# One chunk's residual sum moved: identity matmuls and ScalarE copies in place of VectorE additions

## The chip, the core and the metric

The kernel runs on one core of a Trainium2 chip. The metric is the time of one execution on the device in microseconds (us), the median of the runs shown. The engines are TensorE (PE in the profile, its weight loads PEld), VectorE (DVE), ScalarE (ACT), GpSimd (POOL), and SyncE (SP), which only issues transfers here. "Item 2" below is the third of four chunks; chunks and halves are counted from 0, and "2.1" is chunk 2, half 1.

## The reference, cut to what matters

One layer of a language model on 2 x 1024 tokens of width 256. The token step gathers table rows and adds a low-rank correction chosen by the token's domain. Then come a recurrent attention with 16 heads of 16 x 16 states, and a quantized linear layer, each behind a layer norm and with a residual:

```
h = token_rows + 0.1 * correction(domain)
h = h + attn(layernorm(h))     # state = ret * state + Gamma * (v k^T);  y = (W_static + state) q;  y @ out_w.T + out_b
h = h + ffn(layernorm(h))      # rows scaled to +-127 and rounded, weights likewise, matmul, scales, bias
```

The change concerns the plus sign of the second line, for 512 of the 2048 tokens.

## The kernel before

The tokens go through in four chunks (c = 0 to 3) of 512. In the token-major part of the work a chunk is four tiles of 128 tokens x 256, taken as two halves (h = 0, 1) of two tiles. The running h of the reference lives in SBUF, in `tok` (a view of `tok_dom`, whose rows have 257 elements).

The attention's recurrence is cut into 32 groups g (eight for each chunk, g = 24 to 31 for chunk 3). A group passes through all engines: GpSimd forms the outer products `uu` (L485), TensorE combines them into `w_ps` (L1166), VectorE runs the scan into `e_hg` (L918) and multiplies the states by the queries into `zz` (three quarters at L949, the last quarter at L935), and TensorE collects these into `y_ps` (L1186). For g = 28, 29 and 30 GpSimd makes the larger product in VectorE's place (`assist`, L457 and L460), and it starts the one for g only when TensorE has collected g - 2. `qk`, `pair0`, `pair1` and `fix` (L866, L1060, L876, L1069) treat the lags within a block of four tokens.

When a chunk's eight groups are collected, ScalarE copies `y_ps` into `y_t` (L556), TensorE projects it (`attn`: a bf16 matmul for the bias at L1080, then L1084 and L1098) into one of two PSUM banks, and VectorE adds the result to `tok` (`stats`, step `stat2`, L702), which also frees the bank. For chunks 0 to 2 ScalarE then takes the moments of the new rows (`moments2`: a mean pass at L565, a pass for squares at L570, two tiles each), waits for the bank to be free as the sign that the sum is there, and takes the root (L579). VectorE makes 1/sqrt and the shift (`rstd2`, L721 to L726), ScalarE normalizes (L590), VectorE takes the largest magnitudes (`amax`, L739 to L741), ScalarE scales and rounds (L599, L606), TensorE transposes (`xq_t`, L985), ScalarE copies out (L612), TensorE multiplies (`ffn`, L1112), VectorE scales (L791), and GpSimd adds into `tok` (L431).

Every engine works through its own queue in order. What stands where is written out by hand in calendars of slots, four slots to a group of the recurrence. Around the change they read:

```
PE    108: combine g=27; 109: attn 2.0, attn 2.1; 111: collect g=25; 112: combine g=28; 115: collect g=26, fix 3.0; 116: combine g=29; 117: xq_t 2.0, 2.1; 118: ffn 2.0, 2.1; 119: collect g=27
DVE   107: product g=25 (last), gv1 3.0, stat2 2.0; 108: scan g=27, stat2 2.1; 109: product g=26, rstd2 2.1; 111: product g=26 (last), amax 2.0, 2.1; 112: scan g=28, qk 3.1
ACT   106: q 3.1, moments2 2.0; 107: moments2 2.1; 108: sqrt2 2.1; 112: xhat2 2.0, 2.1; 114: quant 2.0, 2.1; 117: xq_t 2.0
```

Of the kernel before, what the change touches and what calls it, by code (L numbers as in the profile page):

```python
# [21 lines left out]
ACT = mybir.ActivationFunctionType  # L22
# [7 lines left out]
TT = T // P  # L30
NC = TOKENS // T
# [17 lines left out]
ROW = NA * MB  # L49
WAKE = 18  # L50
LAG = 11
AIDED = tuple(range(NC * GROUPS - 4, NC * GROUPS - 1))
NW, NVG, NU, NZ = 2, 4, 3, 2

# [28 lines left out]
    62: base_t 3.1, domain 3.0; 69: base_t 3.0, dom 3.0; 70: y 1.1; 71: moments1 3.0; 74: q 2.1, moments1 3.1, sqrt1  # L83
    3.1; 75: xhat 3.0, xhat 3.1, xhat_t 3.0, moments2 1.0; 76: xhat_t 3.1, moments2 1.1; 77: sqrt2 1.1; 78: v 3.0,
    xhat2 1.0; 80: v 3.1, xhat2 1.1, quant 1.0; 83: k 3.0; 84: k 3.1; 85: xq_t 1.0, quant 1.1, xq_t 1.1; 88: y 2.0;
    93: q 3.0; 101: y 2.1; 106: q 3.1, moments2 2.0; 107: moments2 2.1; 108: sqrt2 2.1; 112: xhat2 2.0, xhat2 2.1;
    114: quant 2.0, quant 2.1; 117: xq_t 2.0; 119: xq_t 2.1; 122: y 3.0; 139: y 3.1, sqrt2 3.0, xhat2 3.0, sqrt2 3.1,
    quant 3.0, xq_t 3.0, xq_t 3.1
"""
DVE_CALENDAR = """  # L90
    -1: w_ret 0.0, w_comb 0.0, mask 0.0, mask 0.1, stat1 0.0, stat1 0.1, rstd1 0.1, first 0.1, xhat_t 0.1, mask 1.0,
# [3 lines left out]
    48: amax 0.0, amax 0.1; 52: qk 1.1; 54: scaled 0.0; 55: scaled 0.1; 56: gv0 1.1; 59: gv1 1.1; 63: qk 2.0; 65: mask  # L95
    3.0; 67: mask 3.1, gv0 2.0; 68: stat1 3.0; 72: stat1 3.1; 73: rstd1 3.1, gv1 2.0, stat2 1.0; 76: stat2 1.1; 79:
    rstd2 1.1; 80: amax 1.0, amax 1.1; 84: qk 2.1; 86: scaled 1.0; 87: scaled 1.1; 88: gv0 2.1; 91: gv1 2.1; 95: qk
    3.0; 97: gv0 3.0; 107: gv1 3.0, stat2 2.0; 108: stat2 2.1; 109: rstd2 2.1; 111: amax 2.0, amax 2.1; 112: qk 3.1;
    115: scaled 2.0; 118: scaled 2.1; 122: gv0 3.1; 123: gv1 3.1; 131: stat2 3.0; 132: rstd2 3.0; 133: stat2 3.1, amax
    3.0; 136: rstd2 3.1, normal 3.1, amax 3.1, whole 3.1, scaled 3.0, scaled 3.1; 138: last_out 3.1  # L100
"""
SP_CALENDAR = """
    -1: copy_v 0.0; 2: copy_v 0.1; 4: copy_k 0.0; 5: read_k 0.0; 7: copy_v 1.0; 9: copy_k 1.0, read_k 1.0; 12: copy_v
# [23 lines left out]
def tower_kernel(nc, ids, table, w_exp, w_proj, w_q, w_k, w_v, b_q, b_k, b_v, w_o, b_o,  # L127
# [14 lines left out]
    def group(g):  # L142

        c, n = divmod(g, GROUPS)
        return c, n, n // NB, n % NB

    with ExitStack() as ctx:
        def sb(name, shape, dt=F32):
            return ctx.enter_context(nc.sbuf_tensor(name, shape, dt))
# [4 lines left out]
        def sem(name):  # L154
            return ctx.enter_context(nc.semaphore(name))
# [31 lines left out]
        idf = sb("idf", [P, P])  # L187
# [13 lines left out]
        tok = tok_dom[:, :, 0:DIM].bitcast(F32)  # L201
        emb_t = sb("emb_t", [P, KD, T])
        act_t = sb("act_t", [P, KD, T])
# [5 lines left out]
        xq_t = sb("xq_t", [P, KD, T], BF16)  # L209
# [13 lines left out]
        start = sb("start", [P, 2, UNITS])  # L223
# [25 lines left out]
        scr_two = [scr[:, i, :].rearrange("p (b d) -> p b d", b=2) for i in range(2)]  # L249
# [21 lines left out]
        s_free = [sem("s_free0"), sem("s_free1"), sem("s_free_w0"), sem("s_free_w1"), sem("s_free_q")]  # L271
# [35 lines left out]
        def filled(eng, name, c, h):  # L307

            bank, before = use[name, c, h]
            eng.wait_ge(s_full[bank], before + 1)  # L310
            return bank
# [11 lines left out]
        def taken(eng, name, c, h):  # L323

            bank, before = use[name, c, h]
            eng.wait_ge(s_free[bank], before + 1)
# [76 lines left out]
        def _(pool):  # L403
# [34 lines left out]
            def after(*_):  # L438

                pool.wait_ge(s_comb, 1)  # L440
# [5 lines left out]
            def assist(_, i):  # L446

                g = AIDED[i]
                c, n, hg, b = group(g)
# [41 lines left out]
        def _(act):  # L491
# [17 lines left out]
            def evacuate(name, dst, reader):  # L509

                def step(c, h):
                    bank = filled(act, name, c, h)
                    if c >= 1 and reader:

                        filled(act, reader[0], c - 1, h if reader[1] is None else reader[1])
                    act.activation(dst[:, :, T // 2 * h:T // 2 * (h + 1)], scr_two[bank], ACT.Copy)\  # L516
                       .then_inc(s_free[bank], 1)
                return step
# [33 lines left out]
            def y(c, hg):  # L552
# [2 lines left out]
                    filled(act, "attn", c - 1, 1)  # L555
                act.activation(y_t[:, hg, :], y_ps[:], ACT.Copy).then_inc(s_yt, 1)  # L556

            def moments(n, name):

                def step(c, h):  # L560
                    taken(act, name, c, h)
                    two = range(2 * h, 2 * h + 2)
                    done = 2 * (c - 1 if n == 0 else c) + h + 1
                    for t in two:
                        last = act.activation(junk[:, 0, t % 2], tok[:, TT * c + t, :], ACT.Copy,  # L565
                                              scale=-1.0 / (HD * DIM), accum_out=mv[:, n, t, 0:1])
                    last.then_inc(s_mean[n], 1)
                    act.wait_ge(s_mean[n], done)
                    for t in two:
                        last = act.activation(junk[:, 1, t % 2], tok[:, TT * c + t, :], ACT.Square,  # L570
                                              bias=mv[:, n, t, 0:1], scale=1.0 / HD, accum_out=mv[:, n, t, 1:2])
                    last.then_inc(s_var[n], 1)
                return step

            def sqrt(n):
                def step(c, h):
                    of, halves_ = tiles(n, c, h)
                    act.wait_ge(s_var[n], 2 * c + h + 1)
                    act.activation(sd[:, n, of], mv[:, n, of, 1], ACT.Sqrt, bias=eps[:]).then_inc(s_sqrt[n], halves_)  # L579
                return step  # L580
# [72 lines left out]
            def dom(c, _):  # L653
                bank = filled(act, "dom", c, 0)
                if c >= 1:
# [2 lines left out]
                act.activation(dom_row[:], row_of[bank], ACT.Copy).then_inc(s_free[bank], 1)  # L658

            stage = {"base_t": evacuate("base_t", emb_t, ("expand", None)), "domain": domain, "dom": dom,  # L660
                     "xhat_t": evacuate("xhat_t", act_t, ("q", 1)), "q": q, "v": v, "k": k, "y": y, "moments1": moments(0, "corr"),
                     "moments2": moments(1, "attn"), "sqrt1": sqrt(0), "sqrt2": sqrt(1),
                     "xhat": xhat(0, tmp_f), "xhat2": xhat(1, tmp_b), "quant": quant, "xq_t": xq_evac,
                     "w_scale": w_scale, "b_scale": b_scale, "sigmoid": sigmoid,
# [7 lines left out]
        def _(dve):  # L672
# [249 lines left out]
            def product(g, last):  # L922
# [5 lines left out]
                if g >= NZ:  # L928
                    dve.wait_ge(s_y, g - NZ + 1)
                if g in AIDED and not last:  # L930
                    return
# [38 lines left out]
        def _(pe):  # L970
            def scratch(name, c, h):

                bank, before = use[name, c, h]
                if before:
                    pe.wait_ge(s_free[bank], before)
                return bank
# [95 lines left out]
            def attn_pre(c, h, bank=None):  # L1072

                if bank is None:
                    bank = scratch("attn", c, h)
                    pe.wait_ge(s_yt, HG * c + 1)
                if c == 0:
                    pe.wait_ge(s_w_back, 80)
                    pe.wait_ge(s_bo, 5)
                pe.matmul(scr_two[bank], rows[:], bo_rows[:].rearrange("p (o d) -> p o d", o=1)  # L1080
                          .to_broadcast([PARTS * 32, 2, DIM]), start=True, stop=False, skip_group_check=True)
                for i in range(2):
                    t = 2 * h + i
                    pe.matmul(scr_two[bank][:, i, :], y_t[:, 0, P * t:P * t + P], wo[:, 0, :],  # L1084
                              start=False, stop=False, skip_group_check=True)

            def attn(c, h):

                if c < NC - 1:
                    bank = scratch("attn", c, h)  # L1090
                    pe.wait_ge(s_yt, HG * (c + 1))
                    attn_pre(c, h, bank)
                else:
                    bank = use["attn", c, h][0]
                    pe.wait_ge(s_yt, HG * (c + 1))
                for i in range(2):
                    t = 2 * h + i
                    last = pe.matmul(scr_two[bank][:, i, :], y_t[:, 1, P * t:P * t + P], wo[:, 1, :],  # L1098
                                     start=False, stop=True, skip_group_check=True)
                last.then_inc(s_full[bank], 1)  # L1100
# [55 lines left out]
            def combine(g):  # L1156

                c, n, hg, b = group(g)
                pe.wait_ge(s_u, 2 * (g + 1))
                if g >= NW:  # L1160
                    pe.wait_ge(s_scan, g - NW + 1)
                else:
                    taken(pe, "expand", 1, g)
                for a in range(NA):
                    for hp in range(NQ):
                        last = pe.matmul(w_ps[32 * hp:32 * hp + 32, g % NW, a], comb[:, NA * n + a, hp],  # L1166
                                         uu[:, g % NU, hp, a], start=True, stop=True, skip_group_check=True)
                last.then_inc(s_w, 1)

            def collect(g):  # L1170
# [7 lines left out]
                for o in range(BLK):  # L1178
                    if o in (0, BLK - 1):
                        if g in AIDED and o == 0:  # L1180
                            pe.wait_ge(s_z_pool, AIDED.index(g) + 1)
                        else:
                            pe.wait_ge(s_z, 2 * g + (2 if o else 1) - sum(a <= g for a in AIDED))
                    for a in range(NA):
# [8 lines left out]
            for slot in SLOTS:  # L1193
                if slot == 0:
                    pe.wait_ge(s_comb, 1)
                if 0 <= slot < NC * UNITS and slot % NA == 0:
                    combine(slot // NA)
                g, late = divmod(slot - LAG, NA)
                if 0 <= g < NC * GROUPS and late == 0:
# [95 lines left out]
```

## Time and profile before

| what | value |
| --- | --- |
| median of 3 runs | 248.78 us (248.72 to 249.97) |
| the profiled execution | 248.81 us |
| its span, first to last instruction | 247.0 us |
| what lies around the span | 1.8 us |
| mean granted TensorE clock | 0.962 |

The trace is of the profiled execution, whose time is within 0.03 us of the median. Times in the rows are microseconds from the span's start unless marked ns. A granted clock of 1.00 is 2.4 GHz and one of 0.50 is 1.2 GHz. In a timeline, a bracket says how long the engine was idle before the piece and what released it; the busy time of a merged piece runs over the pipelined ends of its instructions.

### The profile page before, as it was taken

The page shows a single profiled execution, that of the slowest core. Times are in us where ns is not written, and L with a number is a line of the kernel's source. Part 1 is how long each engine was busy: PE and PEld are TensorE (multiplying, and loading weights), DVE is VectorE, ACT ScalarE, POOL GpSimd, SP SyncE. Part 2 cuts the span into 40 slices and gives each one's busy share as a digit, 9 for nine tenths or more (in the row PEclk, how much of TensorE's full clock was granted, in tenths as well). Part 3 has the DMA queues.
Part 4 walks back from the last instruction along what each step waited for, and adds up shares of the span by engine and source line. Part 5 has one row for each costly group of instructions (what it writes and reads, how often), then busy time and mean ns, then how long its engine had stood idle before and what let it go on. Part 6 is the DMA issues. An engine that isn't in the chain of part 4 may idle for free.

```text
span 247.0 us, 7615 instructions
## 1 busy us (share of the span) xinstructions
PE 217.1 (88%) x3162; PEld 157.4 (64%) x3162; DVE 191.0 (77%) x382; ACT 106.0 (43%) x268; POOL 194.8 (79%) x104
## 2 busy tenths in 40 slices
PE   4997996499899999999989999999897996598871
PEld 4885753376576587685956766859564684266760
DVE  1865761169985986988899969887999997988593
ACT  6403754024532130678851206789510237600240
POOL 4174039999999999999799979496999999679232
PEclk9999999569999999999999999999999999889995
DMA  5492127520044642100564103005642030000202
GB/s 161 125 281 76 45 89 213 152 64 3 21 144 119 181 141 87 45 4 4 163 179 152 65 3 85 4 1 172 165 134 92 3 88 1 4 0 3 88 0 85
DMA packets 19442, 21.24 MB, mean 86 GB/s; under 512 B 2416, under 2 KB 13904, under 8 KB 19408
## 3 DMA queue, kind: packets, MB, share of 16 engines
q1 hardware_dynamic: 18640, 18.65, 25.0%
q0 software_dynamic: 768, 2.11, 3.0%
q8 instruction: 25, 0.41, 0.7%
q14 instruction: 9, 0.07, 0.1%
HBM read 14.98 MB, written 5.77 MB: 84 GB/s over the span
## 4 chain that ended last, share of the span: by engine, by line
PE 61%; DVE 14%; issue 9%; POOL 5%; ACT 5%; DMA 4%; DVEq 0%; POOLq 0%; ACTq 0%
PE y_ps L1186 10%; PE w_ps L1166 10%; PE scr L1031 9%; PE scr L1021 5%; PE scr L1060 5%; PE scr L1045 5%; POOL uu L485 4%; PE scr L985 3%; PE scr L1008 3%; PE y_ps L1177 2%; PE scr L1098 2%; PE scr L1084 2%; DMA tok_dom<-in_table,ids_sb 2%; DVE comb L834 2%; DVE e_hg L918 2%
## 5 line engine op out<-in xcount | busy, mean ns | idle before, releaser
L485 POOL TENSOR_TENSOR uu<-vg,kk 128x1024 f32<-128x1024 f32 x64 | 149.5, 2371 | 22.2 <-DMA vg<-v_far 13.3
L949 DVE TENSOR_TENSOR zz<-e_hg,q_ps 128x1524 f32<-128x1524 f32 x29 | 50.1, 1727 | 0.0
L918 DVE TENSOR_TENSOR_SCAN e_hg<-decay,w_ps 128x512 f32<-128x512 f32 x32 | 38.9, 1216 | 10.4 <-PE w_ps L1166 9.9
L1166 PE MATMUL w_ps<-uu,comb 128*32 128x128 f32 x1024 | 35.9, 279 | 3.7 <-POOL uu L485 3.1
L1166 PEld LDWEIGHTS w_ps<-uu,comb 128*32 128x32 f32 x1024 | 28.0, 111 | 9.8 <-issue 5.3
L1186 PE MATMUL y_ps<-zz,coll 128*32 128x128 f32 x768 | 28.3, 281 | 3.2 <-DVE zz L949 2.4
L1186 PEld LDWEIGHTS y_ps<-zz,coll 128*32 128x32 f32 x768 | 20.0, 111 | 17.1 <-issue 9.9
L409 POOL DMA_INDIRECT tok_dom<-in_table,ids_sb x16 | 15.5, 969 | 11.6 <-DVE comb L834 5.7
L935 DVE TENSOR_TENSOR zz<-e_hg,q_ps 128x512 f32<-128x512 f32 x32 | 21.7, 677 | 0.0
L565 ACT ACTIVATE junk<-tok_dom 128x256 bf16<-128x256 f32 x24 | 9.8, 408 | 26.1 <-DVE tok_dom L702 26.1
L556 ACT ACTIVATE y_t<-y_ps 128x512 f32<-128x512 f32 x8 | 4.8, 598 | 34.9 <-PE y_ps L1186 34.9
L702 DVE TENSOR_TENSOR tok_dom<-scr,tok_dom 128x512 f32<-128x512 f32 x16 | 11.0, 690 | 10.0 <-PE scr L1021 4.9
L1045 PEld LDWEIGHTS scr<-act_t,wk 128*32 128x32 f32 x512 | 13.8, 110 | 5.4 <-issue 5.3
L1060 PE MATMUL scr<-lag,lagw 128*128 128x384 f32 (+2 forms) x48 | 15.3, 432 | 2.2 <-issue 2.2
L1021 PE MATMUL scr<-wproj,mid_t 128*128 128x256 f32 x64 | 17.0, 416 | 0.0
L1045 PE MATMUL scr<-act_t,wk 128*32 128x128 f32 x512 | 16.1, 274 | 0.5 <-issue 0.3
L526 ACT ACTIVATE q_sb<-scr,bq 128x512 f32<-128x512 f32 x8 | 5.5, 688 | 24.7 <-PE scr L1031 24.7
L1031 PE MATMUL scr<-act_t,wv 128*128 128x512 f32 x32 | 15.1, 604 | 0.7 <-ACT act_t L516 0.7
L1031 PE MATMUL scr<-act_t,wq 128*128 128x512 f32 x32 | 15.7, 612 | 0.0
L1021 PEld LDWEIGHTS scr<-wproj,mid_t 128*128 128x128 f32 x64 | 13.1, 208 | 3.9 <-issue 2.2
L1186 PE MATMUL y_ps<-zz,sely 128*32 128x128 f32 x256 | 13.4, 279 | 1.7 <-DVE zz L935 1.7
L423 POOL TENSOR_TENSOR tok_dom<-tok_dom,bf 128x1024 f32<-128x1024 f32 (+1 forms) x5 | 8.9, 1786 | 7.4 <-ACT tmp_b L590 5.6
(134 smaller groups left out, 375.3 us busy)
## 6 DMA issues: line engine op xcount, KB each, us to landing
vg<-v_far SPq DMA_DIRECT2D x32, 256.0 KB, 3.9
v_far<-v_sb SPq DMA_DIRECT2D x8, 256.0 KB, 2.8
out_h<-tok_dom SPq DMA_DIRECT2D x8, 256.0 KB, 2.1
k_far<-kk SPq DMA_DIRECT2D x12, 128.0 KB
k_sb<-k_far SPq DMA_DIRECT2D x4, 384.0 KB, 3.5
wexp<-in_w_exp SPq DMA_DIRECT2D x1, 256.0 KB
tok_dom<-in_table,ids_sb POOLq DMA_INDIRECT x16, 2.8
wproj<-in_w_proj SPq DMA_DIRECT2D x1, 256.0 KB
```

Source lines behind the costliest of these rows:

```text
L409: pool.indirect_dma_start(tok_dom[:, TT * c + t, :], None, table, ix).then_inc(s_base[c][t // 2], 16)
L485: pool.tensor_tensor(uu[:, g % NU, two], v_of.to_broadcast(shape), k_of.to_broadcast(shape), ALU.mult).then_inc(s_u, 1)
L702: dve.tensor_tensor(tok[:, two, :], scr_two[bank], tok[:, two, :], ALU.add).then_inc(s_free[bank], 1)
L918: dve.tensor_tensor_scan(states(g).rearrange("p a m -> p (a m)"), decay[:, NA * n:NA * (n + 1)].rearrange("p a m -> p (a m)"), w.rearrange ...
L935: dve.tensor_tensor(zz[:, g % NZ, :, BLK - 1], states(g), q3, ALU.mult).then_inc(s_z, 1)
L949: dve.tensor_tensor(z, e.to_broadcast(shape), q.to_broadcast(shape), ALU.mult).then_inc(s_z, 1)
L1021: last = pe.matmul(scr_two[bank][:, i, :], mid_t[:, k_, P * t:P * t + P], wproj[:, k_, :], start=(k_ == 0), stop=(k_ == KD - 1))
L1031: last = pe.matmul(scr[:, bank, :], weight[:, k_, P * hg:P * hg + P], act_t[:, k_, :], start=(k_ == 0), stop=(k_ == KD - 1))
L1045: last = pe.matmul(scr[32 * o:32 * o + 32, bank, MB * hp:MB * (hp + 1)], wk[:, k_, w_of], act_t[:, k_, MB * o:MB * (o + 1)], start=(k_ == ...
L1060: last = pe.matmul(scr[:, bank, at:at + n * MB], lagw[:, d, hg, :], lag[:, src:src + n * MB], start=True, stop=True)
L1166: last = pe.matmul(w_ps[32 * hp:32 * hp + 32, g % NW, a], comb[:, NA * n + a, hp], uu[:, g % NU, hp, a], start=True, stop=True, skip_group ...
L1186: last = pe.matmul(y_ps[32 * a:32 * a + 32, MB * o:MB * (o + 1)], w_of, zz[:, g % NZ, a, o], start=False, stop=True, skip_group_check=True)
```

## The change

For chunk 2 alone, VectorE's two additions of `stats(1, "attn")` are left out of its calendar. In their place TensorE adds `tok` inside the accumulation in PSUM: between `attn_pre` and L1098's matmuls it multiplies the identity `idf` by the two tiles of `tok` (128 x 512, f32) into the same bank. ScalarE copies the finished bank into `tok` in a new step `added`, which frees the bank, ahead of the `moments2` of the same half.

```diff
+ADDED = NC - 2
 PE_CALENDAR: unchanged
 ACT_CALENDAR:
-    93: q 3.0; 101: y 2.1; 106: q 3.1, moments2 2.0; 107: moments2 2.1; 108: sqrt2 2.1; 112: xhat2 2.0, xhat2 2.1;
+    93: q 3.0; 101: y 2.1; 106: q 3.1, added 2.0, moments2 2.0; 107: added 2.1, moments2 2.1; 108: sqrt2 2.1; 112:
+    xhat2 2.0, xhat2 2.1;
 DVE_CALENDAR:
-    3.0; 97: gv0 3.0; 107: gv1 3.0, stat2 2.0; 108: stat2 2.1; 109: rstd2 2.1; 111: amax 2.0, amax 2.1; 112: qk 3.1;
+    3.0; 97: gv0 3.0; 107: gv1 3.0; 109: rstd2 2.1; 111: amax 2.0, amax 2.1; 112: qk 3.1; 115: scaled 2.0; 118: scaled
...
+            def added(c, h):
+
+                bank = filled(act, "attn", c, h)
+                act.activation(tok[:, TT * c + 2 * h:TT * c + 2 * h + 2, :], scr_two[bank], ACT.Copy)\
+                   .then_inc(s_free[bank], 1)
...
                     pe.wait_ge(s_yt, HG * (c + 1))
                     attn_pre(c, h, bank)
+                    if c == ADDED:
+                        taken(pe, "corr", c, h)
+                        pe.matmul(scr_two[bank], idf[:], tok[:, TT * c + 2 * h:TT * c + 2 * h + 2, :], start=False,
+                                  stop=False, skip_group_check=True)
```

## Rows read from the trace of the kernel before

**Rows 1.** Page, part 1: busy time, share of the span, instructions.

```profile
PE 217.1 (88%) x3162; PEld 157.4 (64%) x3162; DVE 191.0 (77%) x382; ACT 106.0 (43%) x268; POOL 194.8 (79%) x104
```

**Rows 2.** The chain that ended last, from 199 us: start, us, what.

```profile
200.25 0.88 PE scr L1098 x4
...
201.16 0.70 DVE tok_dom L702
...
201.88 0.92 ACT junk L565 x4
...
202.82 1.10 ACT junk L570 x4
203.92 0.83 ACT junk L565 x4
...
204.77 1.10 ACT junk L570 x4
...
213.39 0.38 PE scr L985 x4
...
215.56 1.87 PE y_ps L1186 x32
```

**Rows 3.** Timeline of TensorE, 199 to 216 us: start, us, what.

```profile
202.04 1.03 PE L1098 MATMUL scr<-wo,y_t 128*128 128x256 f32 x4
...
205.57 0.86 PE L1186 MATMUL y_ps<-zz,coll 128*32 128x128 f32 x24 [0.62 <-DVE zz L949]
207.97 0.43 PE L1186 MATMUL y_ps<-zz,sely 128*32 128x128 f32 x8 [1.53 <-DVE zz L935]
...
213.88 1.69 PE L1112 MATMUL scr<-wf_t,xq_t 128*128 128x256 bf16 x8
```

**Rows 4.** Timeline of VectorE, 201 to 212 us.

```profile
203.10 0.69 DVE L702 TENSOR_TENSOR tok_dom<-scr,tok_dom 128x512 f32<-128x512 f32 x1
...
203.78 1.73 DVE L949 TENSOR_TENSOR zz<-e_hg,q_ps 128x1524 f32<-128x1524 f32 x1
206.29 0.19 DVE L721 RECIPROCAL r_ps<-sd 128x4 f32<-128x4 f32 x1 [0.77 <-ACT sd L579]
...
207.24 0.68 DVE L935 TENSOR_TENSOR zz<-e_hg,q_ps 128x512 f32<-128x512 f32 x1
...
210.78 1.22 DVE L918 TENSOR_TENSOR_SCAN e_hg<-decay,w_ps 128x512 f32<-128x512 f32 x1
```

**Rows 5.** Timeline of GpSimd, 212 to 226 us.

```profile
212.13 0.22 POOL L457 TENSOR_TENSOR zz<-start,q_sb 128x12 f32<-128x12 f32 x1 [2.38 <-DVE e_hg L918]
...
217.81 2.90 POOL L460 TENSOR_TENSOR zz<-e_hg,q_sb 128x1524 f32<-128x1524 f32 x1
222.41 0.22 POOL L457 TENSOR_TENSOR zz<-start,q_sb 128x12 f32<-128x12 f32 x1 [1.70 <-PE y_ps L1186]
```

**Rows 6.** Instructions of L1177 and of L556: duration ns min/median/max, starts.

```profile
L1177 PE MATMUL y_ps<-q_sb,wst x8: 592/592/595, 152.6 to 220.6; 128*128 128x512 f32 x8
L556 ACT ACTIVATE y_t<-y_ps x8: 592/597/613, 77.1 to 228.9; 128x512 f32<-128x512 f32 x8
```

**Rows 7.** The chain again: one f32 matmul of 128x512, as two instructions.

```profile
196.32 0.86 PE y_ps L1177 x2
```

**Rows 8.** TensorE by stretch: length, busy (instructions), granted clock, DMA share, GB/s.

```profile
48.00:50.00 2.00, 1.63 (x3) 0.50 0.46 115
50.00:53.00 3.00, 3.00 (x8) 0.50 0.10 38
...
211.00:214.00 3.00, 0.89 (x10) 1.00 0.00 0
...
214.40:217.80 3.40, 3.32 (x38) 0.50 0.03 7
217.80:221.00 3.20, 3.20 (x40) 1.00 0.00 0
...
241.60:244.00 2.40, 1.01 (x4) 0.52 0.21 77
```

More of the change, by code:

```diff
@@ L85 @@
     xhat2 1.0; 80: v 3.1, xhat2 1.1, quant 1.0; 83: k 3.0; 84: k 3.1; 85: xq_t 1.0, quant 1.1, xq_t 1.1; 88: y 2.0;
-    93: q 3.0; 101: y 2.1; 106: q 3.1, moments2 2.0; 107: moments2 2.1; 108: sqrt2 2.1; 112: xhat2 2.0, xhat2 2.1;
-    114: quant 2.0, quant 2.1; 117: xq_t 2.0; 119: xq_t 2.1; 122: y 3.0; 139: y 3.1, sqrt2 3.0, xhat2 3.0, sqrt2 3.1,
-    quant 3.0, xq_t 3.0, xq_t 3.1
+    93: q 3.0; 101: y 2.1; 106: q 3.1, added 2.0, moments2 2.0; 107: added 2.1, moments2 2.1; 108: sqrt2 2.1; 112:
+    xhat2 2.0, xhat2 2.1; 114: quant 2.0, quant 2.1; 117: xq_t 2.0; 119: xq_t 2.1; 122: y 3.0; 139: y 3.1, sqrt2 3.0,
+    xhat2 3.0, sqrt2 3.1, quant 3.0, xq_t 3.0, xq_t 3.1
 """
@@ L97 @@
     rstd2 1.1; 80: amax 1.0, amax 1.1; 84: qk 2.1; 86: scaled 1.0; 87: scaled 1.1; 88: gv0 2.1; 91: gv1 2.1; 95: qk
-    3.0; 97: gv0 3.0; 107: gv1 3.0, stat2 2.0; 108: stat2 2.1; 109: rstd2 2.1; 111: amax 2.0, amax 2.1; 112: qk 3.1;
-    115: scaled 2.0; 118: scaled 2.1; 122: gv0 3.1; 123: gv1 3.1; 131: stat2 3.0; 132: rstd2 3.0; 133: stat2 3.1, amax
-    3.0; 136: rstd2 3.1, normal 3.1, amax 3.1, whole 3.1, scaled 3.0, scaled 3.1; 138: last_out 3.1
+    3.0; 97: gv0 3.0; 107: gv1 3.0; 109: rstd2 2.1; 111: amax 2.0, amax 2.1; 112: qk 3.1; 115: scaled 2.0; 118: scaled
+    2.1; 122: gv0 3.1; 123: gv1 3.1; 131: stat2 3.0; 132: rstd2 3.0; 133: stat2 3.1, amax 3.0; 136: rstd2 3.1, normal
+    3.1, amax 3.1, whole 3.1, scaled 3.0, scaled 3.1; 138: last_out 3.1
 """
@@ L660, in _ @@
             stage = {"base_t": evacuate("base_t", emb_t, ("expand", None)), "domain": domain, "dom": dom,
-                     "xhat_t": evacuate("xhat_t", act_t, ("q", 1)), "q": q, "v": v, "k": k, "y": y, "moments1": moments(0, "corr"),
+                     "xhat_t": evacuate("xhat_t", act_t, ("q", 1)), "q": q, "v": v, "k": k, "y": y, "moments1": moments(0, "corr"), "added": added,
                      "moments2": moments(1, "attn"), "sqrt1": sqrt(0), "sqrt2": sqrt(1),
```

## The prediction

> **What bounds the kernel now.** I read the page's busy shares first. TensorE leads with 88%, GpSimd and VectorE follow with 79% and 77%, and ScalarE has 43% [rows 1]. By that alone, work that goes from VectorE to ScalarE looks free, but the change also gives TensorE, the fullest engine, two more matmuls. A share is an average, so I then read the chain that ended last around the additions of chunk 2. It runs through exactly this place: TensorE's projection of half 0, VectorE's addition, then all eight moment passes of ScalarE one after another, and from there through the root, the norm and the rounding to the transposes at 213.39 [rows 2]. The reader is to see two things. First, the chain leaves VectorE after *one* addition (0.70 us), and ScalarE's passes follow each other without a gap. The second addition ends at 203.10 + 0.69 = 203.79, before ScalarE gets to its rows at 203.92 [rows 2, 4], so it is hidden. Second, VectorE waits for ScalarE's root: it is idle 0.77 us before L721 [rows 4]. In its queue, behind that wait, stand the last product of g = 26 (TensorE waits 1.53 us for it at 207.97) and the scan of g = 28 (GpSimd waits 2.38 us for it at 212.13) [rows 3, 4, 5]. What makes the root late makes all engines late, and nothing queued between them can run ahead.
>
> **What comes out.** VectorE loses two additions, one of which lies on the chain: 0.70 us. The other is worth nothing by itself. VectorE's product of g = 26 (203.78, 1.73 us) starts some 1.4 us sooner, since 2 x 0.69 us of additions are gone. But TensorE collects that product only behind its own longer queue, and then the freed time runs into the wait for the root, whose idle time of 0.77 us grows by the earlier arrival (1.4) and the later root (1.6, below), to 3.8 us or a little more. So the VectorE time gained is covered by nothing useful; it becomes idle.
>
> **What goes into TensorE.** An identity matmul of 128 x 512 in f32 has the shape of L1177: two instructions, 0.86 us on the chain [rows 7]. (The record of each shows 592 ns, but they overlap [rows 6].) The weight load is hidden under the matmul before, as L1177's is. The bounds are 0.86 and 2 x 0.592 = 1.18 us; the queue is full here, so I take 0.86. Two of them come ahead of the last matmul of half 1: it ends at 202.04 + 1.03 = 203.07 [rows 3], then at 204.79. Half 0 ends at 201.13 + 0.86 = 201.99. The new wait in TensorE's queue is for the bank of `corr` 2.0 and 2.1, which stand in slots 39 and 42, long before 109, and whose rows have been normalized, projected and collected since; it costs nothing.
> The Trainium skill ("TensorE: Matmul & The Clock Gate", section "Back-to-back issue gap") gives about 131 ns for a matmul of 512 columns in a sustained stream and about 216 ns for an isolated one. The row's 0.86 us is four times 0.215, so the trace sides with the second; by the first an identity matmul would be an estimated 0.52 us and the sum some 0.7 us smaller.
>
> **What goes into ScalarE.** `added` is a copy of 128 x 512 f32 from PSUM to SBUF, as L556 is (0.597 us) [rows 6]; I take 0.60 us, with 0.59 and 0.70 (the chain's figure for VectorE's addition, which also walks rows 257 apart) as bounds. Half 0: the copy runs 202.02 to 202.62, its four passes take 0.92 + 0.02 + 1.10 = 2.04 us [rows 2] and end near 204.7. Half 1 of the projection arrives at 204.8, so ScalarE is only just free. The copy ends at 204.83 + 0.60 = 205.43, the passes at 205.45 + 2.04 = 207.49, where they now end at 204.77 + 1.10 = 205.87. **The root comes 1.6 us later.** As a balance: TensorE gives +1.72, the copy of half 1 gives +0.60, and the small slack before ScalarE's second pair, with the sums that fall away, gives back 0.7.
>
> **What the delay does next.** Root, `rstd2`, last product of g = 26, `amax`, scan of g = 28 and rounding all follow in a chain of waits, so TensorE's transposes `xq_t` 2.1 move from 213.39 to 215.0 [rows 2]. Between the projection and there TensorE is often idle now (0.62 and 1.53 us alone in rows 3), and its 1.72 us of extra work costs nothing *there*: it comes to the first part of g = 26 at 205.57 - 0.62 + 1.72 = 206.7, and the last part of g = 26, from VectorE, comes at 207.97 + 1.6. GpSimd's part for g = 28 moves from 212.13 to 213.75. Chunk 2's output path and its stores hang on the same delay but have slack.
>
> **The clock takes part of it back.** The granted clock is 1.00 in 211 to 214, where TensorE is busy 0.89 of 3 us, then falls to 0.50 for 214.4 to 217.8, where TensorE is busy 3.32 of 3.4 us, and is 1.00 again after [rows 8]. That is the dense work: `ffn` 2.0 from 213.88, the collecting of g = 27 (1.87 us at half clock), the pair, the combine. It costs 1.7 us now, half of 3.4, and lies on the chain. With everything 1.6 us later and the fall at the same moment, TensorE meets the low stretch with only `xq_t` 2.1 until 213.88 + 1.6 = 215.5, so 2.3 us of dense work are run slowly, for a loss of 1.15 us. That returns 0.55. GpSimd's product for g = 30 waits for TensorE at 222.41 now, 1.70 us after it was ready [rows 5]; ready moves by 1.6 to 222.3 and TensorE's collecting of g = 28 by 1.6 - 0.55 = 1.05, so TensorE still ends the wait and 1.05 goes on to the end. The last stretch, with half clock for the `ffn` 3.1 after 241.6 [rows 8], stays as it is in this case.
> **Sum:** 248.81 + 1.72 + 0.60 - 0.70 - 0.55 = 249.9 us, the profiled execution's time being 0.03 above the median.
>
> **The rivals.**
> - *The low stretch misses the dense work (no change).* The engine's sparse time now ends 1.6 us later, and the identity matmuls and the combine of g = 29 lie later too. If the clock falls sooner, while TensorE idles, and is back for the `ffn`, or does not fall, the loss of 1.7 us is gone. Then GpSimd bounds: its product for g = 29 ends at 217.81 + 2.90 + 1.6 = 222.3, as late as TensorE lets g = 30 start now (222.41). The time is 248.8, and a full clock at the last `ffn` too would give 0.4 more: 248.4. For it: the pause before the last product of g = 26 grows, from 1.53 to 1.53 + 1.6 - (206.7 - 205.57) = 2.0 us. Against it: 0.50 holds through 48 to 53 although TensorE is busy 1.63 of 2 us and then all of 3 us there [rows 8]; an early fall may not lift in time. The Trainium skill (same page, section "What's actually happening") says that the half clock is the default, released by activity; by that rule the moved pauses matter as much as the moved work, which the falls behind sparse stretches bear out.
> - *The fall moves with the work (slower).* The whole 1.6 stays: 250.4.
> - *The low stretch lasts longer (slower).* TensorE is less busy from 214.4 to 217.8 than it was. If the clock stays at 0.50 for another such stretch of dense work, 1.7 us come on top of 1.05: 251.5. The stretch at 0.50 from 48 to 53 [rows 8] speaks for it.
> - *VectorE's relief wins (faster).* If the identity matmuls and copies were hidden and the chain ran through VectorE, the 1.38 us would come off: 247.4. It decides only if the root is not what VectorE waits for, and its 0.77 us of idle time there [rows 4] says that it is.
>
> **How the numbers follow.** Forecast 42%; low stretch missed 18%; fall moves along 15%; low stretch longer 17%; VectorE's relief 4%; something else 4%. The predicted time is that of the first, 249.9; the case's own range is 249.4 (full clock at the last `ffn`, -0.4) to 250.3 (dearer matmuls or copy). The range from 248.4 to 251.2 takes in the missed stretch and the moved fall and most of the way to the longest; about 0.15 to 0.2 is left out. A measurement tells from no change what is over 0.5%, 1.24 us: faster is below 247.5, slower above 250.0. The forecast lies just inside; 10 of its 42 I put above, together with the two slower rivals: slower 0.44. Same is the other 32 with the missed stretch: 0.51. Faster is 0.05.
>
> **What would show it.** In the changed profile: identity matmuls that add 0.86 us each; the copies at 0.60 us, the second at about 204.8 with ScalarE idle hardly at all before it; L579 just after 207.5 (the last moment pass ends at 205.87 now); VectorE idle some 3.8 us before L721; the last product of g = 26 at 208.9 (207.24 now), `xq_t` 2.1 at 215.0; GpSimd's product for g = 28 at 213.8. If these hold and the time is off, it is the clock: its stretches at 0.50 between 208 and 222 and at the end decide. If L579 moves by less than 1.2 us, the step on TensorE's queue or on ScalarE's copy is wrong; if VectorE does not idle before L721, the whole picture is.

## The result and the profile after

The changed kernel takes 251.75 us (median of 21 runs, 249.75 to 257.13), the kernel before, run beside it, 249.34 us (21 runs, 247.04 to 251.55). The ratio is 1.0084, with a 95% interval of 1.0062 to 1.0106: **slower by 2.1 us, between 1.5 and 2.6**. Forecast were 249.9 us and a loss of 1.1. Single executions of the kernel before spread over 4.5 us; the three shown first had spread over 1.3. Executions more than 1.5% above the fastest of their kernel beside them are left out of the ratios and averages here, which is why the ratio is a little below that of the medians.

The page after, part 1, the line that answers to [rows 1]:

```profile
PE 219.9 (88%) x3166; PEld 159.3 (64%) x3166; DVE 189.8 (76%) x380; ACT 107.4 (43%) x270; POOL 194.9 (78%) x104
```

TensorE has four instructions more, ScalarE two more, VectorE two fewer. The lines of the code have moved: L1091, L1102 and L1109 are the projection with the identity matmul in its middle, L562 is the copy, L572 and L577 the moments, L586 the root. The chain that ended last, from the same place as [rows 2]:

```profile
201.49 0.86 PE scr L1091 x4
202.35 0.86 PE scr L1102 x2
203.21 0.86 PE scr L1109 x4
...
204.29 0.86 PE scr L1091 x4
205.16 0.86 PE scr L1102 x2
206.01 0.88 PE scr L1109 x4
...
206.91 0.61 ACT tok_dom L562
...
207.54 0.92 ACT junk L572 x4
...
208.49 1.10 ACT junk L577 x4
...
209.67 0.31 ACT sd L586
```

The chain no longer leaves TensorE after half 0. It runs through both halves of the projection, both identity matmuls at 0.86 us, and then through the copy and the passes of half 1 alone. That is the path that the prediction drew. From the projection's first matmul (L1091's first record, 201.32) to the root (209.67) it takes 8.35 us; before, from L1084's first record at 199.23 to the root at 205.96, it took 6.73. The difference is 1.62.

VectorE and TensorE around the root, in their timelines, as in [rows 3, 4]:

```profile
210.00 0.19 DVE L728 RECIPROCAL r_ps<-sd 128x4 f32<-128x4 f32 x1 [5.50 <-ACT sd L586]
```

```profile
211.69 0.43 PE L1197 MATMUL y_ps<-zz,sely 128*32 128x128 f32 x8 [2.27 <-DVE zz L942]
```

VectorE's 1.4 us went into idle time, which is now 5.50 us. GpSimd answers to [rows 5]:

```profile
208.94 2.34 POOL L486 TENSOR_TENSOR uu<-vg,kk 128x1024 f32<-128x1024 f32 x1 [0.90 <-PE w_ps L1177]
215.85 0.22 POOL L458 TENSOR_TENSOR zz<-start,q_sb 128x12 f32<-128x12 f32 x1 [4.57 <-DVE e_hg L925]
```

It has one new wait, 0.90 us for the combine of g = 28, that nobody had named. The 4.57 us wait for the scan behind it shows that the new one costs nothing. The clock, by stretch (length, busy, granted clock), as in [rows 8]:

```profile
193.40:196.60 3.20, 3.20 (x42) 0.55 0.02 5
...
213.40:216.70 3.30, 1.63 (x28) 0.50 0.00 0
216.70:220.00 3.30, 2.89 (x24) 0.50 0.02 5
```

Here the two executions differ in a way that the forecast had not allowed for. There is a low stretch *ahead* of the projection, where the program is the same as before, and a longer one behind it. Cut at four points, the two profiled executions compare like this:

| part, us | before | after | difference |
| --- | --- | --- | --- |
| start to the copy y_t 2.1 | 192.95 | 193.77 | +0.82 |
| to the projection's first matmul | 6.28 | 7.55 | +1.27 |
| to the root (the change) | 6.73 | 8.35 | +1.62 |
| to GpSimd's product for g = 30 | 16.45 | 15.94 | -0.51 |
| to the end of the span | 24.59 | 24.59 | 0.00 |

The third line is the forecast's 1.6. The fourth is near its -0.55, but not by the way that was forecast: the low stretch is not the same one at the same moment. It covers 213.4 to 220.0, twice as long as before, and begins 3.7 us behind the root (209.67) where before it began 8.4 us behind it (205.96 and 214.4). The first two lines, 2.1 us of the 3.2 between these executions, lie ahead of the change. So the experiments had two questions: is the later root the cause, and what does the clock do over many executions?

### The profile page after: what moved, and what is told of

Its sections match the earlier page's. It is cut to its first block, busy times and chain, and to the rows that moved or that the text cites. A ratio compares the mean times of both kernels' runs of the same rounds, so it can differ in the third digit from the quotient of the medians.

```text
span 250.2 us, 7623 instructions
## 1 busy us (share of the span) xinstructions
PE 219.9 (88%) x3166; PEld 159.3 (64%) x3166; DVE 189.8 (76%) x380; ACT 107.4 (43%) x270; POOL 194.9 (78%) x104
## 4 chain that ended last, share of the span: by engine, by line
PE 58%; DVE 15%; issue 9%; DMA 6%; POOL 5%; ACT 4%; SPq 1%; DVEq 0%; POOLq 0%; ACTq 0%
PE scr L1038 9%; PE y_ps L1197 9%; PE w_ps L1177 9%; PE scr L1052 5%; PE scr L1067 4%; PE scr L1028 4%; POOL uu L486 4%; PE scr L992 3%; PE scr L1015 3%; PE scr L1109 3%; PE scr L1091 2%; DMA tok_dom<-in_table,ids_sb 2%; PE y_ps L1188 2%; DVE e_hg L925 2%; DVE comb L841 2%
## 5 line engine op out<-in xcount | busy, mean ns | idle before, releaser
L1177 PE MATMUL w_ps<-uu,comb 128*32 128x128 f32 x1024 | 36.5, 282 | 3.7 <-POOL uu L486 3.1
L1177 PEld LDWEIGHTS w_ps<-uu,comb 128*32 128x32 f32 x1024 | 28.5, 112 | 9.7 <-issue 4.7
L572 ACT ACTIVATE junk<-tok_dom 128x256 bf16<-128x256 f32 x24 | 9.8, 408 | 20.9 <-DVE tok_dom L709 20.8
L1067 PE MATMUL scr<-lag,lagw 128*128 128x384 f32 (+2 forms) x48 | 14.7, 419 | 3.4 <-issue 3.4
L709 DVE TENSOR_TENSOR tok_dom<-scr,tok_dom 128x512 f32<-128x512 f32 x14 | 9.7, 690 | 9.1 <-PE scr L1028 4.3
L1028 PE MATMUL scr<-wproj,mid_t 128*128 128x256 f32 x64 | 16.4, 404 | 0.0
```

What stands on the lines that cost most here:

```text
L1028: last = pe.matmul(scr_two[bank][:, i, :], mid_t[:, k_, P * t:P * t + P], wproj[:, k_, :], start=(k_ == 0), stop=(k_ == KD - 1))
L1067: last = pe.matmul(scr[:, bank, at:at + n * MB], lagw[:, d, hg, :], lag[:, src:src + n * MB], start=True, stop=True)
```

## The experiments

To take the clock out, fillers were put where TensorE waits: identity by identity into a scratch bank that is free there.

```diff
+FILL = (7, 6, 5, 5)
...
+            def fill(key, n):
+                bank = scratch(*key)
+                for _ in range(n):
+                    pe.matmul(scr[:, bank, 0:P], idf[:], idf[:], start=True, stop=True)
...
+                    if (name, c) == ("xq_t", 2):
+                        fill((name, c, h), FILL[2 + h])
...
+                    if g == 23 and o == 0:
+                        fill(("q", 3, 1), FILL[0])
+                    if g == 26 and o == BLK - 1:
+                        fill(("xq_t", 2, 0), FILL[1])
```

**First set of fillers, FILL = (14, 12, 11, 10), and the parts of the change alone.** `before_fill` is the kernel before with them, `after_fill` the changed kernel.

> The kernel before with 47 filler matmuls of 128x128 (identity by identity, into a free scratch bank) at four places where TensorE waits between 189 and 214 us: 14 before the collecting of g = 23, 12 before the last part of g = 26, 11 and 10 before xq_t 2.0 and 2.1. They should keep the granted clock at 1.00 until the end of the recurrence. Theory (the clock matters, and where it falls differs between executions): faster than before by 0.7 to 1.7 us, and no stretch at 0.50 between 190 and 222. Rival (the low stretch costs nothing because GpSimd bounds there): no change, 0.0 us. Second rival (the fillers themselves come in the way): slower by up to 1 us.

Measured: ratio to before 1.0136 (1.0085 to 1.0186), slower by 3.4 us. The second rival holds, by more than the 1 us that it gave, and it is a mistake of size. The timeline of TensorE:

```profile
189.67 3.29 PE L982 MATMUL scr<-idf 128*128 128x128 f32 x28
```

14 fillers are 28 instructions and take 3.29 us, about 0.23 us for a filler and not 0.11: an f32 matmul is two instructions here. They ran 1 to 1.4 us past the waits that they were to fill. The set served only for the interval up to the root, which lies ahead of the late ones.

> The changed kernel with the same 47 fillers. With the clock held, only the path to the root is left. Theory (two identity matmuls and one copy on the path, one addition off it): 1.6 us slower than the same fillers without the change. Rival A (the extra 0.5 us of the measured 2.1 belongs to a wait of its own, such as GpSimd's new 0.90 us wait for the combine of g = 28): still 2.1 us slower. Rival B (the loss is mostly the clock's): under 0.8 us slower.

Measured: 1.0183 (1.0123 to 1.0244). Against `before_fill` that is 1.0046, some 1.2 us, uncertain by 1.9, so the time alone separates none of the three expectations. Root 8.35 us behind the projection's start, against 6.73 in `before_fill`.

`pe_only_fill` keeps the identity matmuls and lets VectorE copy:

```diff
-                    dve.tensor_tensor(tok[:, two, :], scr_two[bank], tok[:, two, :], ALU.add).then_inc(s_free[bank], 1)
+                    if (n, c) == (1, ADDED):
+                        dve.tensor_copy(tok[:, two, :], scr_two[bank]).then_inc(s_free[bank], 1)
+                    else:
+                        dve.tensor_tensor(tok[:, two, :], scr_two[bank], tok[:, two, :], ALU.add).then_inc(s_free[bank], 1)
```

> Fillers, and TensorE's part of the change alone: the identity matmuls stay, and VectorE copies the finished bank into tok at the places of its additions (ScalarE has no added step). The sum is complete. Theory: TensorE's 1.72 us is the cause, so 1.5 to 1.7 us slower than the fillers alone, as much as with ScalarE's copies. Rival (ScalarE's copies are what costs): 0.9 to 1.1 us slower, since 0.6 us of copy leaves the path.

Measured: 1.0228 (1.0173 to 1.0284). Root 8.44 us behind the start, 1.71 more than with the fillers alone, as the theory has it. VectorE now waits for each half in its queue (1.97 and 0.78 us idle ahead of its copies). By time it is 2.3 us slower than `before_fill`, uncertain by 1.9. From the root to GpSimd's product for g = 30 the two profiles are alike (18.12 and 18.11 us), so they show no cost beyond the root's.

`act_only_fill` drops the matmul and keeps ScalarE's copies (chunk 2's residual is left out of the sum):

```diff
-                        pe.matmul(scr_two[bank], idf[:], tok[:, TT * c + 2 * h:TT * c + 2 * h + 2, :], start=False,
-                                  stop=False, skip_group_check=True)
```

> Fillers, and ScalarE's part alone: no identity matmuls, ScalarE copies the projection into tok (the residual of chunk 2 is left out of the sum), VectorE adds nothing. Theory: the copy of half 1 adds 0.6 us behind ScalarE's first passes while TensorE's half 1 is ready at 203.1, and the first copy is 0.1 shorter than the addition: 0.5 to 0.6 us slower than the fillers alone. Rival (VectorE's relief is worth something once TensorE pays nothing for it): 0 or faster.

Measured: 1.0131 (1.0074 to 1.0188), the same as `before_fill` within the intervals. Root 7.24 us behind the start, 0.51 more. The profiles say more: from the root to g = 30 it takes 16.84 us, against 18.11 in `before_fill`. VectorE's product comes sooner, TensorE collects the first part of g = 26 at 206.26, 5.54 us behind the projection's start and not 6.34, and the overlong fillers queued behind it start sooner too. So with these fillers VectorE's relief does shorten the path, and this run cannot speak against that rival.

**Fillers of the right size, FILL = (7, 6, 5, 5), and a later root by itself.**

> The kernel before with 23 fillers, 7, 6, 5 and 5 at the same four places. A filler is two instructions of 0.11 us, 0.22 us together, so the first set was twice as long as the waits and held the work up; this set (1.5, 1.3, 1.1, 1.1 us) lies inside the waits of 1.82, 1.53, 1.41 and 1.35 us. Theory (a held clock gives back what the low stretch in the dense work costs): 0.5 to 1.7 us faster than before, and the granted clock at 1.00 from 190 to 222. Rival (the clock's low stretches cost nothing that matters, or GpSimd bounds): no change within 0.3 us.

Measured: 0.9969 (0.9936 to 1.0003). In its profile the clock stays at 1.00 from 190 to 222, as the theory had it, the root comes 6.73 us behind the start, and from the root to g = 30 it takes 15.28 us, where [rows 8]'s low stretch made it 16.45. That stretch cost 1.17 us, not 1.7: about 15.28 us remain at full clock. Over many executions the gain is 0.8 us, with an interval from 1.6 down to nothing, so it is not clear of noise.

> The changed kernel with the same 23 fillers. Theory (1.6 us later root, and the other 0.5 us of the measured 2.1 is lost at low clock): 1.6 us slower than the same fillers without the change (0.65%). Rival (the 0.5 is a wait of the change itself): 2.1 us slower (0.85%).

Measured: 1.0019 (0.9982 to 1.0056), against `before_fill2` 1.0050, or 1.2 us, uncertain by 1.25: the time excludes neither the theory's 1.6 nor the rival's 2.1. The profile decides. Root at 8.35, then 15.28 to g = 30: with the clock held, the change's whole mark is the 1.62 us before the root.

`act_delay` is the kernel before with a later root and nothing else:

```diff
+                    if (n, c, h) == (1, NC - 2, 1):
+                        for i in range(LATER):
+                            act.activation(y_copy[:], y_t[:, 0, :], ACT.Copy).then_inc(s_late, 1)
+                            act.wait_ge(s_late, i + 1)
```

> The kernel before, with three dummy copies of 128x512 on ScalarE between the last moment pass of chunk 2 and its root, each waiting for the one before: the root comes 1.8 to 1.9 us later and nothing else is changed, VectorE's additions and TensorE's work as before. Theory (the whole loss is the later root, whatever makes it late): slower by 1.8 us plus what the clock adds, so as slow as the changed kernel or up to 0.4 us more. Rival (TensorE's own extra work matters beyond the root): clearly less than the changed kernel, 1 us or under.

Measured: 1.0090 (1.0056 to 1.0124), 2.2 us slower (1.4 to 3.1). ScalarE's timeline:

```profile
206.30 1.94 ACT L578 ACTIVATE y_copy<-y_t 128x512 bf16<-128x512 f32 x3
208.32 0.30 ACT L586 ACTIVATE sd<-mv,eps 128x4 f32<-128x4 f32 x1
```

The root is 8.56 us behind the projection's start, 1.83 more than before. A later root, without any extra work on TensorE and with VectorE's additions in place, costs as much as the change, within the intervals. This is the experiment that carries the cause.

> The changed kernel as it is, on the same chip beside the others. Theory and rivals: 2.1 us slower than before, within 1.5 to 2.6, and the root 8.35 us after the projection's first matmul (L1091), where it is 6.73 in the kernel before; only the clock's stretches at 0.50 should lie elsewhere than in the first profile.

Measured: 1.0136 (1.0078 to 1.0195), 3.4 us (1.9 to 4.9), more than expected, though the interval reaches into 1.5 to 2.6. The root is at 8.35, and again there is a low stretch ahead of the projection.

**Where the clock matters.** `before_late` and `after_late` have FILL = (0, 6, 5, 5), `after_early` and `before_early` (7, 0, 0, 0). `best1` adds to `before_fill2` the other two places where the clock is low in the profile of before:

```diff
+                if g == 1:
+                    fill(("pair0", 0, 0), 12)
...
+                    if (i, c, hg) == (0, 0, 0):
+                        fill(("pair0", 0, 0), 8)
...
+                if c == NC - 1:
+                    wake(1, 3)
```

> The kernel before with only the fillers behind the changed place: 6 before the last part of g = 26 and 5 before each of the two xq_t. Theory (low stretches behind the changed place cost about 1 us each when they fall on the dense work there, in some executions): 0.2 to 1.2 us faster than before, granted clock 1.00 from 205 to 222. Rival (what the 23 fillers gained came from the seven ahead of g = 23): no change.

Measured: 0.9995 (0.9954 to 1.0035): no change, as the rival has it, but from 1.1 us faster to 0.9 slower all is possible, and most of the theory's 0.2 to 1.2 with it.

> The changed kernel with the same 16 late fillers. Theory (the changed kernel's longer pause behind the projection draws more low clock onto the dense work than before, about 0.5 us on average): 1.5 to 1.7 us slower than before_late, and faster than the changed kernel by more than before_late is faster than before. Rival (the excess comes from the low stretch at 192 to 198 seen in two profiles of the changed kernel, ahead of the change): still 2.1 us or more slower than before_late.

Measured: 1.0042 (1.0007 to 1.0078); against `before_late` 1.0047, or 1.2 us, uncertain by 1.3. That is nearer to the theory; the rival's 2.1 is not excluded.

> The changed kernel with only the 7 fillers ahead of g = 23. Theory: about as slow against before as the changed kernel itself, 1.7 to 2.3 us, since the pauses behind the projection are left open. Rival: the early fillers take the excess away, so 1.5 us or less against before.

Measured: 1.0043 (1.0011 to 1.0076), 1.1 us slower than before. The rival holds: seven fillers ahead of g = 23 take away about as much as the late ones. In its profile there is still a stretch of 3.4 us at half clock, from about 210.4 to 213.8, and it costs nothing: 15.27 from the root to g = 30. That is what the prediction's first rival, the low stretch that misses the dense work, had described.

> The kernel before with the 23 fillers, and three more sets at the other two places where the granted clock is 0.50 in the profile of before: 12 before the combine of g = 1 (a wait of 3.11 us for GpSimd at 41.1), 8 before pair0 0.0 (a wait of 2.23 us at 46.1), and 3 before each ffn of chunk 3 (waits of 0.78 us). Theory: the chain runs over TensorE at half clock from 44 to 54, where 7.5 us of busy time would take 3.7, so with the 23 fillers' gain 3 to 5 us faster than before. Rival (the transfers and GpSimd bound there as soon as TensorE is faster): 0.5 to 1.5 us faster.

Measured: 0.9988 (0.9955 to 1.0020). The granted clock was 0.996 on average, and the time is no shorter than with the 23 fillers alone (0.9969), nor measurably than before. The chain that ended last shows why:

```profile
40.70 3.48 DMA k_far<-kk
...
44.19 3.66 DMA k_sb<-k_far
...
47.94 1.10 DVE lag L867 x3
...
49.08 0.91 PE scr L1070 x2
```

Between 40 and 48 us the round trip of the keys through memory is what ends last; the low clock there lay under it. What TensorE gained behind it (L1060's two instructions took 1.62 us at half clock, L1070's take 0.91) did not reach the end. The rival's bound by transfers is nearer, and even its 0.5 us is not seen (the interval reaches to 1.1). No version that beats both kernels beyond the interval was found.

**More draws.** `after_p1` to `after_p3` are the changed kernel again, `before_p1` and `before_p2` the kernel before.

> The changed kernel, one more profile, to see where the granted clock is 0.50 this time. Theory (where the low stretches fall is chance; behind the projection the changed kernel draws more of them): no low stretch at 190 to 200 in at least one of the new profiles of the changed kernel, and one at 208 to 224 in most. Rival (the changed kernel somehow always meets one ahead of its projection): one at 190 to 200 again, so the matmuls L1038 to L1091 start over 7 us after y_t, where they start 6.28 after it at full clock.

> The kernel before, one more profile. Theory: a low stretch at 208 to 222 in some executions only, and at 190 to 198 as often as in the changed kernel. Rival: never one at 190 to 198.

> As after_p1. In each, the root comes 8.35 us after the projection's first matmul; from the root to GpSimd's product for g = 30 it takes 15.3 us at full clock and up to 16.5 where a low stretch covers the dense work.

> As before_p1. The root comes 6.73 us after the projection's first matmul; the second interval as in after_p2.

Measured in one execution each: 252.15 and 254.85 us changed, 248.72 and 247.83 before. By part, with the profiles that bear on it:

| kernel | to y_t | to projection | to root | to g = 30 | to end |
| --- | --- | --- | --- | --- | --- |
| before | 192.95 | 6.28 | 6.73 | 16.45 | 24.59 |
| before_p1 | 192.91 | 6.28 | 6.73 | 16.35 | 24.63 |
| before_p2 | 193.54 | 6.28 | 6.72 | 15.29 | 24.17 |
| act_delay | 193.48 | 6.28 | 8.56 | 15.56 | 24.22 |
| after | 193.77 | 7.55 | 8.35 | 15.94 | 24.59 |
| after_again | 194.70 | 7.91 | 8.35 | 16.21 | 24.63 |
| after_p1 | 193.21 | 7.21 | 8.35 | 17.34 | 24.19 |
| after_p2 | 195.96 | 7.92 | 8.34 | 16.21 | 24.67 |
| after_late | 193.12 | 6.28 | 8.35 | 15.27 | 24.28 |

Three rows that make the fourth column (length, busy, clock), the first of `before_p2`, the others of `after_p1`:

```profile
209.00:212.00 3.00, 3.00 (x34) 0.50 0.01 3
```

```profile
212.00:218.00 6.00, 4.28 (x48) 0.51 0.00 0
218.00:222.00 4.00, 4.00 (x41) 0.50 0.02 6
```

In `before_p2` the low stretch fell on about 208.7 to 212.1, ahead of a wait of TensorE's, and cost nothing; in `after_p1` it lasted 10 us and cost 2.06. The root's interval never moves by more than 0.02. The last column is 24.6 where the half clock covers the last `ffn` and 24.2 where it does not: the 0.4 us that the prediction gave for it.

By their own test the four expectations go to the rival: both new profiles of the changed kernel have a low stretch ahead of the projection (7.21 and 7.92 us), and neither of the kernel before has one. The 17.34 us of `after_p1` also lies above the 16.5 that they allowed.

At full clock TensorE is not what the chain behind the root runs through for most of the way. In `before_p2` it stays on VectorE, through the product of g = 27 and the scaling of chunk 2's output, and reaches TensorE late, so part of what TensorE loses at half clock is covered:

```profile
217.93 0.86 DVE tmp_b L791 x2
...
218.83 0.92 PE scr L1060 x4
```

GpSimd still waits 0.60 us for TensorE ahead of g = 30 there.

> The kernel before with only the 7 fillers ahead of g = 23. In four profiles of the changed kernel the clock was at 0.50 for 3.4 us between 191 and 200, ahead of the projection, at a price of 0.9 to 1.6 us; in three of the kernel before it was not. If that is so in general, the early fillers gain 1 us or more in the changed kernel (after_early: 1.0 us slower than before, against 2.1) and nothing here: 0.0 to 0.3 us. Rival (the kernel before meets that low stretch as often, and the profiles are chance): 0.5 to 1.0 us faster than before.

Measured: 1.0004 (0.9965 to 1.0043): nothing, as the theory said. The interval is 1.0 us to either side, so the rival's 0.5 is not excluded.

> The changed kernel once more, beside before_early. Theory: 2.1 to 2.5 us slower than before, a low stretch at 190 to 200 in its profile again. Rival (chance): none there, and the projection starts 6.28 us after y_t.

Measured: 1.0058 (1.0017 to 1.0099), 1.4 us, under the theory's 2.1 to 2.5, with an interval (0.4 to 2.5) that takes them in. Its profile (an execution of 253.46 us) has no low stretch ahead of the projection, which starts 6.28 us behind y_t, as the rival had it, and one of 10 us behind the root.

The averages over the executions of this study agree with the parts. The time at half clock follows from each run's mean granted clock m as 2 x (1 - m) x span. The kernel before has 18.4 us of it (90 runs, mean 248.9 us), the changed kernel 20.7 (32 runs, `after_p2` among them, 251.4), `act_delay` 22.2 (12 runs, 251.2), `after_fill2` 14.2 (249.9) and `before_fill2` 14.5 (248.4).

## Why the prediction was wrong

The time, 251.75, lies 0.55 us above the range, and the loss of 2.1 us is about twice the one forecast. Step by step:

- **"The chain runs through exactly this place", and "the root comes 1.6 us later": right.** 0.86 us for each identity matmul, 0.60 for the copy, 2.04 for the passes, 8.35 instead of 6.73 us to the root in every profile of the changed kernel (8.34 once). TensorE's part alone gives 1.71, ScalarE's alone 0.51. They do not simply add: with the matmuls in place half 1 comes so late that its sum lies on the path whichever engine makes it, VectorE in 0.69 us or ScalarE in 0.60, hence 8.44 and 8.35. The Trainium skill ("TensorE: Matmul & The Clock Gate", section "Back-to-back issue gap") gives 131 ns for a 512-column matmul in a stream and 216 ns for an isolated one. The trace does not agree with the first for this f32 work: 0.86 us inside a full queue is four times 0.215.
- **"It becomes idle": right, a little mis-sized.** VectorE idles 5.50 us before `rstd2` where 3.8 was forecast. With the clock held the same wait is 3.99 us (`after_fill2`), so the forecast was nearly right; the other 1.5 go with TensorE's half clock ahead of the projection, which holds the projection up and not VectorE.
- **"What makes the root late makes all engines late": right.** `act_delay` shows it alone: a root later by 1.83 us costs 2.2 us.
- **"The clock takes part of it back": this step failed.** It assumed that "the fall [is] at the same moment", so that the work moves out of it and 0.55 us return. Between the two profiled executions the part behind the root did come out near it (-0.51), but by luck: the fall began earlier against the work and lasted twice as long. But the moment differs from execution to execution: in three of the kernel before the part behind the root took 16.45, 16.35 and 15.29 us, in four of the changed kernel 15.94, 16.21, 17.34 and 16.21, on average 0.4 more and not 0.55 less, and a low stretch can also come ahead of the projection. Over many executions the clock returns nothing. The changed kernel spends 2.3 us more at half clock, `act_delay` 3.8 more, and the loss is the 1.62 us of the root plus about 0.5. How large that rest is stays uncertain: 1.62 itself lies in the interval of 1.5 to 2.6, while the forecast's 1.1 does not. With fillers that hold the clock the change costs 1.2 us (three pairs: 1.0046, 1.0050, 1.0047, uncertain by 0.008, 0.005 and 0.005), which agrees with 1.62 within its uncertainty and gives no sign of a further wait.
- **The price of the low stretch, 1.7 us, was too high:** 16.45 - 15.28 = 1.17. TensorE's lost 1.7 us were not all on the path, because at full clock VectorE leads the chain up to 218.8 (`before_p2`); no profile shows less than 15.27 behind the root.
- **The rivals.** "The low stretch lasts longer" had the right sign and the right engine, and happened in some executions (`after_p1`, 10 us); it gave a loss of 2.75, and over many executions it is 2.1. "VectorE's relief" is excluded by the 5.50 us of idle time and by `after_fill2`, where the root is 1.62 us later and nothing behind it is shorter than in `before_fill2`. "The low stretch misses the dense work" happened in single executions (`after_early`), but its bound was too low: at full clock TensorE, not GpSimd, still ends the wait for g = 30, by 0.61 us in `after_fill2`. "The fall moves with the work", 250.4, is nearest to the mean effect, a loss of 1.6 against 2.1.
- The range was drawn around one execution, 248.81, while the kernel before has a median of 249.34 in 21 runs. Half a microsecond of the miss, nearly all of the distance to the range, is that alone. The loss, 2.1 against 1.1, is not touched by it.

**What stays open.** The four profiles of the changed kernel in the table that have no fillers have a low stretch ahead of the projection (0.9 to 1.6 us), the three of the kernel before have none, nor have `act_delay` and `before_late`, although the program there is the same in all of them. Early fillers help the changed kernel (from 1.0084 to 1.0043, in different sets of runs whose intervals overlap) and not the kernel before (1.0004), which speaks for a difference; `after_late` and `after_p3` had none there, and the four profiled executions (252.06 to 254.85 us) are slower than the changed kernel's median, which speaks for chance. What would cause it is not shown. The excess over 1.62 us is therefore put down to TensorE's time at half clock, but not to one place, and that it is the clock rests on the averages and is not shown by itself.

## What to carry to other kernels

Moving work from a fuller engine to an emptier one by busy share can lose: ask which engine's *chain* the work joins. Here VectorE's second addition was hidden, while TensorE's two matmuls and ScalarE's copy all went in front of the same root, and VectorE's gain turned into waiting for it. And do not bank a gain on where the clock is low in one trace: read the parts that repeat in every execution (here to 0.02 us) as the forecast, and give the clock a range.

## What was unexpected of the hardware

- The same program has its stretches at half clock at different times in different executions, one of 3.4 us behind the root costing from 0.0 (`before_p2`, from 208.7) to 1.17 us (before, at 214.4). Longer pauses of TensorE go with more of them: 18.4 us in the kernel before, 22.2 with a root later by 1.83 us.
- Holding the clock up is not worth much by itself: `best1` raised the mean granted clock from 0.962 to 0.996 and the time stayed within 0.9955 to 1.0020 of before.
